# Turning softmax probabilities by DMA block exchange and VectorE instead of TensorE in a perceiver block

## What is computed

```
x = x + softmax(layernorm(x) @ ctx^T) @ ctx        # x 256 x 2048, ctx 25088 x 2048
x = x + attn(layernorm(x))                          # over the heads, 32 query heads, 8 key/value heads
x = x + ffn(layernorm(x))                           # x @ W_base^T (2048 x 2048) + b, and top-2 of 8 low-rank experts
```

## Time and profile before

| | |
|---|---|
| median of 3 runs | 2474.45 us (2474.32 to 2477.35) |
| the profiled execution | 2480.7 us, span 2478.9 us |
| PE busy | 2444.7 us, 99% |
| DVE busy | 1966.2 us, 79% |
| POOL busy | 1412.2 us, 57% |
| ACT busy | 1098.5 us, 44% |
| SP's DMA queue | 424136 packets, 477.23 MB, 79.0% of 16 engines |
| mean granted TensorE clock | 0.996 |

### The profile page before, as it was taken

One profiled execution on the slowest core, in us unless ns is written; L12 is line 12 of the kernel. 1 busy time (PEld: TensorE's weight loads), 2 busy tenths in 40 slices (PEclk: granted clock), 3 DMA queues, 4 the chain that ended last, 5 costly groups with the idle time before them and its releaser, 6 DMA issues. The chain is left out here.

```text
span 2478.9 us, 36112 instructions
## 1 busy us (share of the span) xinstructions
PE 2444.7 (99%) x11446; PEld 2013.8 (81%) x11446; DVE 1966.2 (79%) x2706; ACT 1098.5 (44%) x1577; POOL 1412.2 (57%) x1052
## 2 busy tenths in 40 slices
PE   6999999999999999999999999999999999999999
PEld 5888888888888888888888888888888888877777
DVE  8888788787888888888888888888888888874456
ACT  4444444444444444444444444444444444433543
POOL 2766666666665655655566565556556555651541
PEclk9999999999999999999999999999999999999999
DMA  9988878888789888889888988888888898789642
GB/s 231 257 221 213 233 203 230 218 208 230 205 231 230 213 204 219 217 220 217 209 220 206 226 217 203 219 223 210 215 217 220 214 216 215 201 187 189 173 119 90
DMA packets 434167, 519.80 MB, mean 210 GB/s; under 512 B 66886, under 2 KB 308550, under 8 KB 431688
## 3 DMA queue, kind: packets, MB, share of 16 engines
q1 hardware_dynamic: 424136, 477.23, 79.0%
q0 software_dynamic: 9984, 41.95, 5.2%
HBM read 488.71 MB, written 30.41 MB: 209 GB/s over the span
## 5 line engine op out<-in xcount | busy, mean ns | idle before, releaser
L621 POOL TENSOR_TENSOR nat_lo<-raw,nat_hi 128x512 fp32r<-128x512 f32 x784 | 1171.0, 1524 | 862.7 <-ACT nat_hi L781 829.7
L1085 DVE TENSOR_TENSOR ch_lo<-tr,ch_hi 128x512 fp32r<-128x512 f32 x784 | 762.6, 973 | 295.5 <-ACT ch_hi L770 291.7
L770 ACT CAST ch_hi<-tr 128x512 fp32r<-128x512 f32 x784 | 481.3, 621 | 797.7 <-PE ps L1493 777.3
L1491 PE MATMUL ps<-ch_hi,xt_hi 128*128 128x512 f32 x1696 | 671.7, 396 | 9.3 <-DVE ch_lo L1085 5.1
L1493 PE MATMUL ps<-ch_hi,xt_lo 128*128 128x512 f32 x1696 | 662.1, 390 | 0.0
L1492 PE MATMUL ps<-ch_lo,xt_hi 128*128 128x512 f32 x1696 | 661.5, 390 | 0.0
L1491 PE MATMUL ps<-nat_hi,pt_hi 128*128 128x512 f32 x1568 | 610.4, 389 | 0.0
L1493 PE MATMUL ps<-nat_hi,pt_lo 128*128 128x512 f32 x1568 | 610.3, 389 | 0.0
L1492 PE MATMUL ps<-nat_lo,pt_hi 128*128 128x512 f32 x1568 | 610.0, 389 | 0.0
L1081 DVE STREAM_TRANSPOSE tr<-quart 128x512 f32<-128x512 f32 x784 | 547.5, 699 | 2.4 <-DMA quart<-in_ctx_dram 2.2
L781 ACT CAST nat_hi<-raw 128x2048 fp32r<-128x2048 f32 x196 | 374.4, 1910 | 207.5 <-PE ps L1493 186.2
(11 more groups left out here) (202 smaller groups left out, 1387.0 us busy)
## 6 DMA issues: line engine op xcount, KB each, us to landing
quart<-in_ctx_dram SPq DMA_DIRECT2D x392, 512.0 KB, 8.4
raw<-in_ctx_dram SPq DMA_DIRECT2D x196, 1024.0 KB, 8.2
wq_in<-in_L_attn_Wq_dram POOLq DMA_DIRECT2D x16, 1024.0 KB, 6.3
win<-in_L_ffn_W_base_dram SPq DMA_DIRECT2D x64, 256.0 KB, 6.8
tr<-wt_dram POOLq DMA_DIRECT2D x64, 256.0 KB, 3.6
wt_dram<-stage SPq DMA_DIRECT2D x32, 256.0 KB, 5.6
wt_dram<-stage_b SPq DMA_DIRECT2D x32, 256.0 KB, 10.3
wq_dram<-wq_out POOLq DMA_DIRECT2D x16, 256.0 KB, 2.3
```

The lines of the kernel that those rows point to most:

```text
L621: last = pool.tensor_tensor(nat_lo[:, j, t], raw[:, j % 2, t], nat_hi[:, j, t].bitcast(F32), ALU.subtract)
L770: act.copy(ch_hi[:, c % RING_CH, :], tr[:, c % RING_TR, :]).then_inc(chunk_hi, 1)
L1085: dve.tensor_tensor(ch_lo[:, c % RING_CH, :], tr[:, c % RING_TR, :], ch_hi[:, c % RING_CH, :].bitcast(F32), ALU.subtract).then_inc(chunk_s ...
L1491: pe.matmul(out_, a_hi, b_hi, start=start, stop=False)
```

## The change

`probs` is no longer turned by PE in turns 2 to 48. ACT writes the exponents with their 32-key blocks regrouped; SP moves them, 4 DMAs for each q (64 KB each, 512 bytes a run), into a new tile `quads` so that 32x32 blocks stand where the transposed tile wants them; DVE turns the blocks back into `probs`; ACT and DVE make `pt_hi` and `pt_lo` from there, no longer from PSUM. Turn 1 and the group after the last turn stay on PE. Pieces 0 and 1 stand one chunk later on PE, DVE's first adds and ACT's first row piece too. `quads` lies where `b_nat` is loaded, so all 8 `b_nat` DMAs go behind the last `pt_lo`. `win` of row block m is loaded in step 0 of its own pair, behind the first `quart` half, not at the end of the pair before; the fifth part of `win` is turned at c = 10 and no longer at c = 14 of step 1.

```diff
@@ -162,6 +162,7 @@
+        quads = put(at_b, "quads", [P, TT, QR, P])
@@ -384,6 +386,7 @@
+                self.by_dma = not (self.first or self.second or self.over)
@@ -411,7 +414,7 @@
-        PIECE_AFTER = {5: 0, 7: 1, 9: 2, 11: 3, 13: 4, 15: 5}
+        PIECE_AFTER = {6: 0, 8: 1, 9: 2, 11: 3, 13: 4, 15: 5}
@@ -485,11 +488,22 @@
+            def move_probs(turn, q):
+                sp.wait_ge(probs_ready, turn.times(TT, q + 1 - TT))
+                for b in range(QR):
+                    sp.dma_start(quads[b * SQ:(b + 1) * SQ, q], probs[:, q, b * P:(b + 1) * P]).then_inc(probs_moved[q], 16)
             def next_block(turn, m=None):
                 step = turn.step if m is not None else None
+                if turn.by_dma:
+                    for q in range(TT):
+                        move_probs(turn, q)
                 quarter = ctx_quarter
                 next_quarters(turn, 0, quarter(turn.times(KB, KB), 0))
+                if step == 0:
+                    load_win(m)
...
                 for j in range(2):
+                    if j == 1 and step == 1:
+                        sp.wait_ge(wt_stored[4], m * 16 + 16)
                     sp.wait_ge(nat_ready[j], turn.times(1, 1))
                     load_rows(j + 2, ctx_rows(turn.times(KB), j + 2))
...
-                if step == 1:
-                    for k in (3, 4):
-                        sp.wait_ge(wt_stored[k], m * 16 + 16)
-                    load_win(m + 1)
...
             next_block(REST[0], LAST_M)
-            for e in range(EXPERTS // 2):
-                load_expert(e)
...
             last_row0 = REST[1].times(KB)
+            for q in range(TT):
+                move_probs(REST[1], q)
...
             sp.dma_start(x_nat[:], x_dram).then_inc(x_again, 16)
-            for e in range(EXPERTS // 2, EXPERTS):
+            sp.wait_ge(lo_drained, G_PT + TT * (NB - 1))
+            for e in range(EXPERTS):
                 load_expert(e)
@@ -784,14 +796,22 @@
+                if turn.by_dma:
+                    to = to.rearrange("p (b t j) -> p t b j", b=QR, t=KT)
+                    of = of.rearrange("p (t b j) -> p t b j", b=QR, t=KT)
...
             def probs_group(turn, q):
+                if turn.by_dma:
+                    act.wait_ge(out_ready, turn.times(8, 6 + q + 1 - 16))
+                    hi_group(turn.times(TT, G_PT + q - TT), q, pt_hi[:, q], probs[:, q].rearrange("p (t m) -> p t m", t=KT))
...
-            ROWS = {11: 0, 15: 1}
+            ROWS = {12: 0, 15: 1}
@@ -1133,12 +1153,19 @@
+            def turn_probs(turn, q):
+                dve.wait_ge(probs_moved[q], turn.times(16 * QR, -16 * QR))
+                dve.transpose(probs[:, q].rearrange("p (t i a) -> p t a i", t=KT, a=QR),
+                              quads[:, q].rearrange("p a (t j) -> p t a j", t=KT)).then_inc(group_done, 1)
...
-            ADD_AFTER = {9: 0, 11: 1, 13: 2, 15: 3, 17: 4}
+            ADD_AFTER = {10: 0, 12: 1, 13: 2, 15: 3, 17: 4}
@@ -1549,6 +1579,8 @@
+                elif turn.by_dma and v < TT:
+                    pe.wait_ge(lo_drained, turn.times(TT, G_PT - 1 + v))
@@ -1576,7 +1608,7 @@
-                    if c == (3 if turn.second else 1) and not turn.first:
+                    if c == 3 and turn.second:
                         for q in range(TT):
                             probs_group(turn, q)
@@ -1820,7 +1852,7 @@
-TURN_AFTER = {(0, 8): 0, (0, 12): 1, (0, 16): 2, (1, 4): 3, (1, 14): 4}
+TURN_AFTER = {(0, 8): 0, (0, 12): 1, (0, 16): 2, (1, 4): 3, (1, 10): 4}
```

More of the change, by code:

```diff
@@ L311, in perceiver_block @@
         probs_ready = sem("probs_ready")
+        probs_moved = [sem(f"probs_moved{q}") for q in range(TT)]
         alpha_ready = sem("alpha_ready")
@@ L457, in load_win @@
                     sp.dma_start(win[a * SQ:(a + 1) * SQ],
-                                 w_base[bass.ds(m * P, P), a * QF:(a + 1) * QF].rearrange("(r j) x -> j r x", j=SQ)
+                                 w_base[bass.ds((m + 1) * P - P, P), a * QF:(a + 1) * QF].rearrange("(r j) x -> j r x", j=SQ)
                                  ).then_inc(win_loaded, 16)
@@ L518, in _ @@
             sp.wait_ge(wq_stored, 16 * DC)
-            load_win(0)
             in_w_pairs(sp, next_block)
@@ L786, in softmax @@
                 act.wait_ge(max_ready, turn.times(TT, q + 1))
-                act.activation(probs[:, q, :], ps[:, SCORE_BANK + TT * new + q, :], ACT.Exp,
+                to, of = probs[:, q, :], ps[:, SCORE_BANK + TT * new + q, :]
+                if turn.by_dma:
+                    to = to.rearrange("p (b t j) -> p t b j", b=QR, t=KT)
+                    of = of.rearrange("p (t b j) -> p t b j", b=QR, t=KT)
+                act.activation(to, of, ACT.Exp,
                                bias=neg_max[:, new, q:q + 1],
@@ L793, in probs_group @@
             def probs_group(turn, q):
-                hi_group(turn.times(TT, G_PT + q - TT), q, pt_hi[:, q], bank4(q))
+                if turn.by_dma:
+                    act.wait_ge(out_ready, turn.times(8, 6 + q + 1 - 16))
+                    hi_group(turn.times(TT, G_PT + q - TT), q, pt_hi[:, q], probs[:, q].rearrange("p (t m) -> p t m", t=KT))
+                else:
+                    hi_group(turn.times(TT, G_PT + q - TT), q, pt_hi[:, q], bank4(q))
             def row_piece(turn, j):
@@ L1134, in add_late_piece @@
                                          ALU.mult, ALU.add).then_inc(acc_updated, 1)
+            def turn_probs(turn, q):
+                dve.wait_ge(probs_moved[q], turn.times(16 * QR, -16 * QR))
+                dve.transpose(probs[:, q].rearrange("p (t i a) -> p t a i", t=KT, a=QR),
+                              quads[:, q].rearrange("p a (t j) -> p t a j", t=KT)).then_inc(group_done, 1)
             def probs_group(turn, q):
-                lo_group(turn.times(TT, G_PT + q - TT), pt_lo[:, q], bank4(q), pt_hi[:, q])
-            ADD_AFTER = {9: 0, 11: 1, 13: 2, 15: 3, 17: 4}
+                src = probs[:, q].rearrange("p (t m) -> p t m", t=KT) if turn.by_dma else bank4(q)
+                lo_group(turn.times(TT, G_PT + q - TT), pt_lo[:, q], src, pt_hi[:, q])
+            ADD_AFTER = {10: 0, 12: 1, 13: 2, 15: 3, 17: 4}
             ADD_LATE_AFTER = {3: 5, 5: 6, 7: 7}
@@ L1165, in iteration @@
                     lo_chunk(turn.times(DC, c), c)
+                    if c in ADD_LATE_AFTER and lagging:
+                        add_late_piece(turn, ADD_LATE_AFTER[c])
+                    if c == (7 if turn.second else 5) and not turn.first:
+                        if turn.by_dma:
+                            for q in range(TT):
+                                turn_probs(turn, q)
+                        for q in range(TT):
+                            probs_group(turn, q)
                     n = c + AHEAD
@@ L1168, in iteration @@
                         transpose_chunk(turn.times(DC, n), n, turn.times(16 * QR, 16 * QR * (n // DC)))
[L1169 to L1173, removed]
                     if c == 7 and not turn.first:
```

## The result

The changed kernel is slower: 2490.98 us median (2488.08 to 2494.43, 5 runs) against 2474.45 (2471.07 to 2478.28, 5 runs) of before, ratio 1.0069, 95% interval 1.0055 to 1.0082. The forecast was 2460 us, in a range of 2434 to 2492: the time lies in the range, but the change costs 16.5 us where it was to save 14.5. The profiled execution took 2490.98 us, span 2489.4.

A forecast was written before the change was run, and what follows sets the result against it. PE was taken as the bound, nearly every microsecond a PE instruction. Transposes gone -42.8, `win` wait +22.1 and end +6.2 sum to -14.5 us: 2460 us against the median 2474.45, range 2434 to 2492 (8 in 10).

The forecast's parts named there:

- The saving, 42.8 us: PE in turns 2 to 48: eight transposes fewer per turn, 0.91 us each of 47 turns, all of it counting.
- Moves and turnings at 0 in every turn: Probabilities' moves on SP and turnings on DVE: covered before chunk 6 is due on PE, so costed at 0.
- rival 2: Probabilities late in every turn, PE waits before chunk 6: 1.3 us x 47, 2521 us; at half, 2490; chance 0.23.
- The step-0 wait, 1.4 us: 16 W turns of step 0: DVE stands for late `win`, PE waits 1.4 us before piece 2, 22.1 us in all.
- The turning with its 16-byte step: DVE's turning of probabilities writes at a four-element step: between 0.6 us, the dense time, and twice that.
- rival 3: Turnings writing at 16-byte steps take twice as long, 1.3 us more on DVE in 47 turns: 2474, no change; chance 0.15 with its like.
- the 1.3 us of slack: DVE subtracts chunk 6 by 1036.5, PE needs it at 1037.8: 1.3 us of slack, so PE waits for nothing.
- The tail, 6.2 us: Behind the last turn: four more `b_nat` DMAs delay a `raw` piece 7.8 us; less 1.6 slack, PE waits 6.2.

The follow-up runs named there:

- experiment 8: Experiment 7's kernel with turn 2's probabilities turned on TensorE again, as before the change: 2438.79 us, ratio 0.9878 to the kernel before.
- Experiment 1: The changed kernel with `win` loaded ahead of the `quart` loads in step 0: 2448.91 us, ratio 0.9894 to the kernel before.
- experiment 7: Experiment 1's kernel with SP's wait for the stored `Wq` moved from ahead of the W loop to ahead of `load_win`: 2449.03 us, ratio 0.9905.
- experiments 5 and 6: 5: the changed kernel with `win` between third and fourth quarter load, 2452.6 us; 6: the changed kernel with turnings written densely (probabilities in wrong order), 2487.11 us.
- experiment 4: The kernel before with only the `win` load moved behind its own pair's quarter half, fifth part's store wait ahead of the last `raw` piece: 2476.44 us, ratio 1.0009.
- experiment 3: The changed kernel with `win` loaded at its old place, the end of step 1, ahead of the moves: 2523.39 us, ratio 1.0196 to the kernel before.

## Why the prediction was wrong

- **The saving, 42.8 us: right.** The period is 43.52, and with the obstacles cleared (experiment 8) all but 1.2 us of it arrives.
- **Moves and turnings at 0 in every turn: right for 45 turns, and the first step that failed.** "Nothing is queued behind them that was issued before 1029.79, so this costs SP nothing": this asked who stands behind the moves, in one W turn, and not what SP stands at when the moves come up. In turn 2 that is a `raw` load, in turn 17 the wait for `Wq`; there the moves go out 3 us late. I had priced rival 2 as a thing of all 47 turns or none. In turn 2 its mechanism cost 8.6 us, and experiment 8 takes it away. In turn 17 it cost 1.2 itself; the late moves also held `win` back, which made the rest of the 8.5. Experiment 1 brings turns 17 and 18 to 3.1, experiment 7 to 0.0.
- **The step-0 wait, 1.4 us: the right wait, too small a size.** The due time was right: by the forecast's own sum the wait begins when `win` comes 22.96 - 1.4 = 21.56 us into the turn; experiments 5 and 6 put it at 21.3. The landing was not: taken 22.96, measured 23.66 on average. An issue of a move takes 0.64 us and not the 0.48 of a large load, and the chain of issues hands this on to `win`, which is issued 8.9 us into the turn and not 8.3. That this is what makes it land 0.7 later is read from the timelines; no run changes the issue time alone. 0.7 more and 0.2 for the slower restarts make 2.3: 32.5 us over 14 turns, not 19.6.
- **The turning with its 16-byte step: rival 3 had the direction right and the consequence wrong.** It took 1.08 against 0.68 us, 1.6 times and not twice. Of the 1.3 us of slack, two such turnings use 0.8. The rule on float32 steps (the Trainium skill, SBUF — State Buffer, "Door 1: The DMA port swizzle") agrees with these rows. The step lengthened the turning and not the kernel.
- **The tail, 6.2 us: the right wait, half the size.** It was 3.0 us, with the slower matmuls behind it about 5. The eight `b_nat` issues held SP for 18.3 us; the `raw` piece was issued 1.0 us behind the last softmax start and no longer 4.2 ahead of it, 5.2 later where I took 7.8. Against the trace of before, the end as a whole is not longer; against that of experiment 4 it is, by 7.2, and TensorE's wait for POOL's `ch_lo` grew in it too, to 2.1 us from 0.4 before. What the end costs stays open.
- **The clock was in no term.** The three long waits (5.5, 4.6 and 3.0 us) were each followed by matmuls at 0.43 us; the step-0 waits of 1.22 and 0.95 were not, nor was the 1.9 of turn 47. This made the one-off stalls dear: 2.9 of turn 2's 8.6 us, 2.6 of turn 17's 8.5.
- **The range held by chance.** The 2490 us that stands in rival 2 is for a landing that is late in every turn, by half of its way. No such lateness was there: turns 3 to 16, but for turns 4 and 7, and those of step 1 lose next to nothing.

The unforeseen terms are 12.9 + 2.7 us in the step-0 turns 19 to 47, 8.6 in turn 2, 7.1 in turn 17, 2.1 in turns 3 to 16. These 33.4 turn -14.5 into +18.9, if the tail costs the 6.2 forecast; the medians say +16.5. The two profiled executions say +10.5, because there start and end together came out 2.8 shorter instead of 6.2 longer.

## What to carry to other kernels

Where a queue works in order, the place of an added transfer is priced twice, by what stands behind it and by what the queue stands at when its turn comes, and that in the first turn of each loop as well as in the steady one. A wait on an engine with slack costs nothing up to a point and then microsecond for microsecond, so two edits that each use part of the slack must be summed before they are called free. The cheapest repair here was one line: the load of `win`, due 21.3 us into the turn, went ahead of four that are due later.

## What the runs showed of the hardware

- A stream transpose of 128x512 that writes with a step of four float32 took 1.08 us, written densely 0.68.
- 64 KB moved within SBUF landed in 2.7 us (median), 6.7 with 1 MB of `win` ahead of it in the queue. SP took 0.64 us for each issue of such a move in the turn shown, against 0.48 for the larger loads.
- TensorE behind an idle of 2.8 us ran 8 matmuls at 0.43 us, behind one of 5.5 us 12, at a granted clock of 0.50 to 0.55 in those stretches; behind idles of 0.8 to 1.1 us only the first matmul was slower, 0.33 instead of 0.23. It is not certain from the length of the idle: of 14 idles of 2.7 to 3.2 us in experiment 3, 12 were followed by such matmuls and 2 were not.
